# Turning attention's z and y rows with transposing transfers from SBUF to SBUF

## What is computed

```python
def _L0_xattn_ref(x, context, ...):           # 16 heads of 64, 77 keys a batch
    xn = _layernorm(x, ln_gamma, ln_beta)
    q = (xn @ w_q).reshape(B, SQ, NUM_HEADS, DIM_HEAD)
    k, v = jnp.split(context @ w_kv, 2, axis=-1)
...
    attn = jax.nn.softmax(jnp.einsum('bqhd,bkhd->bhqk', q * SCALE, k), axis=-1)
    out = jnp.einsum('bhqk,bkhd->bqhd', attn, v).reshape(B, SQ, INNER)
    return (out @ w_out + b_out) * jnp.tanh(gate[0])
def _L0_ffn_ref(inputs, gate_w, gate_b, expert_w, expert_b):
    gate_probs = jax.nn.softmax(x @ gate_w.T + gate_b, axis=-1)   # 8 experts and 2 null ones
    weights, selected = jax.lax.top_k(gate_probs, 2)
...
x = x + jnp.tanh(g_xattn[0]) * _L0_xattn_ref(_layernorm(x), ctx, ...)
x = x + jnp.tanh(g_ffn[0]) * _L0_ffn_ref(_layernorm(x), ...)
```

## Time and profile before

| | |
|---|---|
| median of 3 runs | 1773.74 us |
| the runs | 1767.39, 1773.74, 3117.3 us |
| span of the profiled execution | 1768.9 us |
| PE busy | 1483.3 us (84%) |
| DVE busy | 1438.9 us (81%) |
| POOL busy | 1089.4 us (62%) |
| ACT busy | 827.5 us (47%) |
| DMA queue of SP / of POOL, share of 16 engines | 23.5% / 13.0% |

### The profile page before, as it was taken

One profiled execution on the slowest core, in us unless ns is written; L12 is line 12 of the kernel. 1 busy time (PEld: TensorE's weight loads), 2 busy tenths in 40 slices (PEclk: granted clock), 3 DMA queues, 4 the chain that ended last, 5 costly groups with the idle time before them and its releaser, 6 DMA issues. The chain is left out here.

```text
span 1768.9 us, 38608 instructions
## 1 busy us (share of the span) xinstructions
PE 1483.3 (84%) x10329; PEld 815.2 (46%) x10330; DVE 1438.9 (81%) x3838; ACT 827.5 (47%) x1289; POOL 1089.4 (62%) x1029
## 2 busy tenths in 40 slices
PE   5675899999999999999999999999169998777775
PEld 3321455555555555555555555555034444333332
DVE  6766779999899999899999999997657777566664
ACT  6755454544544544554544544444134444333432
POOL 0620556766666766666766666665456665677775
PEclk9877999999999999999999999999579999899999
DMA  5986222132322142322132322111344443455553
GB/s 183 229 195 189 69 82 76 59 137 80 111 80 74 60 137 79 112 80 74 60 137 78 114 80 80 61 61 55 120 125 147 145 139 115 133 176 171 181 165 109
DMA packets 116661, 201.62 MB, mean 114 GB/s; under 512 B 23699, under 2 KB 51475, under 8 KB 115848
## 3 DMA queue, kind: packets, MB, share of 16 engines
q1 hardware_dynamic: 88520, 129.99, 23.5%
q0 software_dynamic: 28096, 71.08, 13.0%
HBM read 120.75 MB, written 83.07 MB: 115 GB/s over the span
## 5 line engine op out<-in xcount | busy, mean ns | idle before, releaser
L710 PE MATMUL mix<-u_sb,pT 128*128 128x512 f16 (+1 forms) x1920 | 429.8, 382 | 67.8 <-ACT pT L808 62.2
L676 PE MATMUL scores<-m_sb,zT 128*128 (+2 forms) x2304 | 413.7, 339 | 5.0 <-ACT zT L788 3.4
L1440 PE MATMUL out_bank<-w_parts,y_columns 128*128 x1440 | 335.6, 384 | 0.0
L710 PEld LDWEIGHTS mix<-u_sb,pT 128*128 128x128 f16 (+1 forms) x1920 | 184.3, 98 | 292.8 <-issue 76.2
L676 PEld LDWEIGHTS scores<-m_sb,zT 128*128 128x128 f16 x2304 | 224.3, 98 | 176.7 <-issue 8.3
L793 ACT ACTIVATE expd<-expd 128x385 f32<-128x385 f32 (+1 forms) x192 | 105.0, 547 | 325.1 <-DVE expd L891 325.1
L1462 ACT COPY y_columns<-yT_bank 128x1024 f16<-128x1024 f16 x120 | 121.5, 1012 | 245.9 <-PE yT_bank L1430 245.9
L1116 POOL DMA_INDIRECT table<-payload,row_i x128 | 192.9, 1507 | 44.6 <-issue 31.8
L1440 PEld LDWEIGHTS out_bank<-w_parts,y_columns 128*128 128x128 f16 x1440 | 137.5, 99 | 145.9 <-issue 6.7
L1380 POOL DMA_INDIRECT got_ring<-x_mid,token x120 | 127.0, 1058 | 96.4 <-DVE token L1493 67.8
L1430 PE MATMUL yT_bank<-ident,y_rows_parts 128*128 128x128 f16 x960 | 74.5, 221 | 107.2 <-issue 59.2
(11 more groups left out here) (147 smaller groups left out, 2644.2 us busy)
## 6 DMA issues: line engine op xcount, KB each, us to landing
x_ln<-in_x_dram SPq DMA_DIRECT2D x64, 256.0 KB, 2.6
x_res<-in_x_dram SPq DMA_DIRECT2D x64, 256.0 KB, 2.9
x_mid<-x_out SPq DMA_DIRECT2D x64, 256.0 KB, 2.1
out_dram<-x_out SPq DMA_DIRECT2D x64, 256.0 KB, 2.4
w_raw<-in_L_ffn_expert_w_dram SPq DMA_DIRECT2D x64, 128.0 KB, 2.6
m_dram<-m_stage SPq DMA_DIRECT2D x32, 231.0 KB, 5.2
u_dram<-m_sb SPq DMA_DIRECT2D x48, 154.0 KB
m_sb<-m_dram SPq DMA_DIRECT2D x3, 2464.0 KB, 9.0
```

The source lines that it names most:

```text
L676: last = pe.matmul(scores[k][:, 0:n], zT[:, s, zp, t, :], m, start=(t == 0 and (zp, mp) == PRODUCTS[0]), stop=(t == DT - 1 and (zp, mp) == ...
L710: last = pe.matmul(mix[:], pT[0:n, k, pp, :], u_sb[0:n, k, up, :], start=(k == 0 and (pp, up) == PRODUCTS[0]), stop=(k == KT - 1 and (pp, ...
L1440: last = pe.matmul(c.out_bank[s][:], yT[:, s, yp, t, :], w_parts[:, bass.ds(e, 1), t, wp, :].rearrange("p a n -> p (a n)"), start=(t == 0 ...
```

## The change

Both turns leave PE and ACT. SP issues one transposing transfer for z (`turn_z`) and one for y (`turn_y`) in each step, straight from `z_parts` and `y_parts` to `zT` and `yT` in SBUF, each for both parts at once; each raises one of two semaphores, by the tile's parity. `yT` gets a second buffer, and `zT_bank` goes. `score` and `gate` wait for these semaphores, and so do `split_z` and `split_y` before they write the parts again. `turn_z(i + 1)` and `turn_y(i - 3)` stand at the head of SP's step i. The first steps of the first batch are written out, since they have no y yet.

```diff
--- before.py
+++ after.py
@@ -440,7 +440,7 @@
         x_spread = sb("x_spread", [P, 2, 1])
         y = sb("y", [P, 2, D])
         y_parts = sb("y_parts", [P, 2, 2, D], F16)
-        yT = sb("yT", [P, 2, DT, P], F16)
+        yT = sb("yT", [P, 2, 2, DT, P], F16)
         gate_raw = sb("gate_raw", [P, DT, GATES])
         gate_scaled = sb("gate_scaled", [P, DT, GATES])
         gate_parts = sb("gate_parts", [P, DT, 2, GATES], F16)
@@ -480,7 +480,6 @@
         pT_bank = [psum(f"pT_bank{k}", [P, 4, 2, P], F16) for k in range(3)]
         gate_bank = pT_bank[2][:, 2:4].rearrange("p a b c -> p (a b c)").bitcast(F32)[:, 0:GATES]
         rank_bank = pT_bank[2][:, 2:4].rearrange("p a b c -> p (a b c)").bitcast(F32)[:, 16:16 + TOP_K * EXPERTS]
-        zT_bank = psum("zT_bank", [P, 2, DT, P], F16)
         mix = psum("mix", [P, D])
 
         affine_in = sem("affine_in")
@@ -500,8 +499,7 @@
         affine_done = sem("affine_done")
         z_hi_ready = sem("z_hi_ready")
         z_lo_ready = sem("z_lo_ready")
-        zT_summed = sem("zT_summed")
-        zT_ready = sem("zT_ready")
+        zT_in = [sem(f"zT_in{s}") for s in range(2)]
         scores_ready = sem("scores_ready")
         top_ready = sem("top_ready")
         less_ready = sem("less_ready")
@@ -525,8 +523,7 @@
         y_ready = sem("y_ready")
         y_hi_ready = sem("y_hi_ready")
         y_lo_ready = sem("y_lo_ready")
-        yT_summed = sem("yT_summed")
-        yT_ready = sem("yT_ready")
+        yT_in = [sem(f"yT_in{s}") for s in range(2)]
         gate_summed = sem("gate_summed")
         logits_ready = sem("logits_ready")
         choosing = sem("choosing")
@@ -587,11 +584,39 @@
                 sp.dma_start(w_raw[:, s, :], w_rows[bass.ds(i // 2, 1), s].rearrange("a p n -> (a p) n")).then_inc(
                     w_in[s], 16)
 
+            def turn_z(i, s):
+                sp.wait_ge(z_hi_ready, i + 1)
+                sp.nop(nofuse=True)
+                sp.wait_ge(z_lo_ready, i + 1)
+                sp.nop(nofuse=True)
+                if later(i, 2):
+
+                    sp.wait_ge(scores_ready, 3 * (i - 1))
+                sp.nop(nofuse=True)
+                sp.dma_start_transpose(out=zT[:, s].rearrange("p l t q -> p (l t) q"),
+                                       in_=z_parts[:, s].rearrange("p l d -> p (l d)")).then_inc(zT_in[s], 16)
+
+            def turn_y(i, s):
+                sp.wait_ge(y_hi_ready, i + 1)
+                sp.nop(nofuse=True)
+                sp.wait_ge(y_lo_ready, i + 1)
+                sp.nop(nofuse=True)
+                if later(i, 2):
+
+                    sp.wait_ge(gate_summed, i - 1)
+                sp.nop(nofuse=True)
+                sp.dma_start_transpose(out=yT[:, s].rearrange("p l t q -> p (l t) q"),
+                                       in_=y_parts[:, s].rearrange("p l d -> p (l d)")).then_inc(yT_in[s], 16)
+
             def store(i, s):
                 sp.dma_start(rows(x_mid, i), x_out[:, s, :]).then_inc(stored[s], 16)
                 sp.dma_start(rows(x_final, i), x_out[:, s, :]).then_inc(stored[s], 16)
 
-            def step(i, s, more=True, before=True):
+            def step(i, s, more=True, before=True, turns=True, turns_y=True):
+                if turns:
+                    turn_z(i + 1, 1 - s)
+                if turns_y:
+                    turn_y(i - 3, 1 - s)
                 if before:
 
                     sp.wait_ge(x_out_ready, i - 1)
@@ -617,13 +642,17 @@
 
 
                 i0 = b * TPB
-                step(i0, 0, before=not first)
+                step(i0, 0, before=not first, turns_y=not first)
                 if not first:
                     sp.wait_ge(mix_ready, i0)
                     for load in load_u(sp, u_sb, u_dram, b):
                         load.then_inc(u_in, 16)
-                step(i0 + 1, 1, before=not first)
-                with sp.Fori(0, TPB // 2 - 3) as q:
+                step(i0 + 1, 1, before=not first, turns_y=not first)
+                if first:
+                    step(2, 0, turns_y=False)
+                    for n in range(3, 6):
+                        step(n, n % 2)
+                with sp.Fori(2 if first else 0, TPB // 2 - 3) as q:
                     for k in range(2):
                         step(i0 + 2 * q + 2 + k, k)
                 if not last:
@@ -631,38 +660,29 @@
                         sp.wait_ge(scores_ready, 3 * i0)
                     load_m(sp, m_sb[:, bass.ds((b + 1) % 2, 1)], m_dram, b + 1).then_inc(m_in, 16)
                 for k in range(4):
-                    step(i0 + TPB - 4 + k, k % 2, more=not last)
+                    step(i0 + TPB - 4 + k, k % 2, more=not last, turns=not last or k < 3)
 
             for i in range(2):
                 sp.wait_ge(z_ready, i + 1)
                 load_x_ln(i + 2, i)
+            turn_z(0, 0)
             batch(0, first=True)
             with sp.Fori(1, BATCH - 1) as b:
                 batch(b)
             batch(BATCH - 1, last=True)
             for i in range(TILES - 2, TILES):
+                turn_y(i - 1, (i - 1) % 2)
                 sp.wait_ge(x_out_ready, i + 1)
                 store(i, i % 2)
+            turn_y(TILES - 1, (TILES - 1) % 2)
             for s in range(2):
                 sp.wait_ge(stored[s], 32 * TILES // 2)
 
         @block.tensor
         def _(pe):
-            def transpose_z(i, s):
-
-                pe.wait_ge(z_hi_ready, i + 1)
-                pe.wait_ge(z_lo_ready, i + 1)
-                pe.wait_ge(zT_ready, i)
-                if later(i, 4):
-                    pe.wait_ge(yT_ready, i - 3)
-                for part in range(2):
-                    for t in range(DT):
-                        last = pe.transpose(zT_bank[:, part, t, :], z_parts[:, s, part, t * P:(t + 1) * P], ident16[:])
-                last.then_inc(zT_summed, 1)
-
             def score(i, s):
 
-                pe.wait_ge(zT_ready, i + 1)
+                pe.wait_ge(zT_in[s], 8 * (i - s) + 16)
                 if later(i, TPB):
                     pe.wait_ge(m_in, 16 * (i // TPB))
                 for k in range(3):
@@ -712,18 +732,8 @@
                                              stop=(k == KT - 1 and (pp, up) == PRODUCTS[-1]))
                 last.then_inc(mix_ready, 1)
 
-            def transpose_y(i, s):
-                pe.wait_ge(y_hi_ready, i + 1)
-                pe.wait_ge(y_lo_ready, i + 1)
-
-                pe.wait_ge(zT_ready, i + 4 if not isinstance(i, int) or i + 4 <= TILES else TILES)
-                for part in range(2):
-                    for t in range(DT):
-                        last = pe.transpose(zT_bank[:, part, t, :], y_parts[:, s, part, t * P:(t + 1) * P], ident16[:])
-                last.then_inc(yT_summed, 1)
-
-            def gate(i):
-                pe.wait_ge(yT_ready, i + 1)
+            def gate(i, s):
+                pe.wait_ge(yT_in[s], 8 * (i - s) + 16)
                 if isinstance(i, int) and i == 0:
                     pe.wait_ge(gate_split, 3)
 
@@ -734,7 +744,7 @@
                 pe.wait_ge(pT_ready, 3 * (i + 3) if not isinstance(i, int) or i + 3 <= TILES else 3 * TILES)
                 for t in range(DT):
                     for yp, gp in PRODUCTS:
-                        last = pe.matmul(gate_bank, yT[:, yp, t, :], gate_parts[:, t, gp, :],
+                        last = pe.matmul(gate_bank, yT[:, s, yp, t, :], gate_parts[:, t, gp, :],
                                          start=(t == 0 and (yp, gp) == PRODUCTS[0]),
                                          stop=(t == DT - 1 and (yp, gp) == PRODUCTS[-1]))
                 last.then_inc(gate_summed, 1)
@@ -757,18 +767,13 @@
                     score(i, s)
                 if live(i - 1):
                     transpose_p(i - 1)
-                if live(i + 1):
-                    transpose_z(i + 1, 1 - s)
                 if live(i - 1):
                     mix_values(i - 1)
                 if live(i - 5):
                     rank(i - 5, 1 - s)
                 if live(i - 3):
-                    gate(i - 3)
-                if live(i - 2):
-                    transpose_y(i - 2, s)
-
-            transpose_z(0, 0)
+                    gate(i - 3, 1 - s)
+
             run(pe, step)
 
         @block.scalar
@@ -776,16 +781,10 @@
             def split_z(i, s):
 
                 act.wait_ge(affine_done, 2 * i + 2)
-                if not isinstance(i, int) or i >= 2:
-                    act.wait_ge(zT_summed, i - 1)
+                if later(i, 2):
+                    act.wait_ge(zT_in[s], 8 * (i - s))
+                    act.nop(nofuse=True)
                 act.copy(z_parts[:, s, 0, :], z[:, s, :]).then_inc(z_hi_ready, 1)
-
-            def copy_zT(i, s):
-                act.wait_ge(zT_summed, i + 1)
-                if not isinstance(i, int) or i >= 2:
-
-                    act.wait_ge(scores_ready, 3 * (i - 1))
-                act.copy(zT[:, s], zT_bank[:]).then_inc(zT_ready, 1)
 
             def exponent(i, s, k):
```

(14 more changed lines are left out.)

## The result

The changed kernel takes 1805.61 us, median of 4 runs (1803.24 to 1810.26), beside 1770.57 for the kernel before, run with it. The ratio is 1.0209, 95% interval 1.018 to 1.0238: slower, though the interval doesn't settle whether by more than 2%. The profiled execution spans 1804.4 us, against 1768.9 before, so 35.5 us are to be found.

What follows compares the result with a forecast made beforehand. The prediction took DVE to bound the attention stage. From the 1768.9 us trace span, 41 us for held steps and 5 us at the stage's ends gave 1815 us, own range 1805 to 1830, whole range 1755 to 1850.

Steps and rivals of the forecast that it cites:

- What bounds: Attention stage: DVE sets the pace, PE and ACT follow with about 1 us slack; direct gain 0 to 3 us.
- PE as the bound: Rival, attention stage: PE bounds, so 1.22 us a step come back whole or half; 1730 us at half; chance 0.05.
- The cast and z_low: Attention step: earlier ACT cast starts POOL's z_low 0.13 us before DVE's L1026, held; net 0.73 to 0.83 us a step.
- the rival by which a wait ahead of the cast makes it late by more than 0.13 us: Attention step: z_low starts after L1026, no stall, L975's 0.15 us a step won; 1766 us; chance 0.27.
- The transfers: SP's queue, z and y each step: 2 to 5 us each, hidden behind 16 us of slack, price 0.
- SP's issue: SP, each transposing transfer: about 0.4 us to issue, like its other issues, hidden, price 0.
- The slow rival: Attention stage: each transposing transfer takes 9.7 us, costing 7.2 us a step, 461 us, giving 2230; chance 0.20.
- The sum: Whole kernel: trace span 1768.9, plus 41 us for steps and 5 us at the stage's ends, gives 1815 us.
- some steps at batch starts not hit: Attention stage: z_low falls 0.2 to 0.5 us later against DVE there, so 55 of 64 steps were taken as hit.
- the steps' term: Attention stage: 55 held steps at 0.75 us each, 41 us in all.

Runs made afterwards that it cites:

- y alone: Kernel before with only y sent by a transposing transfer and no yT copy on ACT, z still turned by PE: 1822.28 us, ratio 1.0.
- early cast: Kernel before with two ACT calls exchanged, the cast of z ahead of the copy of zT, no transposing transfer: 1857.37 us, ratio 1.0179.
- filler: Changed kernel plus an unread ACT copy of about 1 us where the zT copy stood, transfers kept: 1827.79 us, ratio 1.002.
- placed pair: Changed kernel and kernel before, each with POOL's y_low waiting for row_i_ready and z_low for inverse_ready: ratios 0.9705 and 0.9738.
- placed kernel: Changed kernel with POOL's y_low waiting for row_i_ready and z_low for inverse_ready: 1788.59 us, ratio 0.9705.

## Why the prediction was right, step by step

**What bounds.** DVE did: PE's wait for pT grew to 2.2 us a step, as said (118.1 us over 52 waits), y alone won nothing an ordinary step, and each 0.16 or 0.87 us taken from DVE's list came back in the step. The prediction had PE as the bound at 0.05; it is not, save at a few batch starts (below).

**The cast and z_low.** Foreseen: z_low 0.13 us ahead of L1026, a stall to z_low's end, L975 freed, step up by 0.73 to 0.83 us. Measured: 0.13 us, 1.03 us long, L975 at 0.16, step up by 0.70. The early cast alone gave the same, and the rival by which a wait ahead of the cast makes it late by more than 0.13 us fell: the cast started 0.27 us after the copy ahead, as was read from the earlier trace rows.

**The transfers.** Foreseen 2 to 5 us and hidden: 3.2 us and hidden, as the filler shows. SP's issue was mis-sized, 1.23 us for 0.4, three times too low; it cost nothing in the stage, because SP is idle for most of a step. The slow rival's 9.7 us, as the usual price of a transfer, are seen nowhere: the longest landing of a y is 5.8 in the changed kernel, and y alone has one of 9.8 beside a median of 3.1. What the DMA engines moved, by slices of 0.225 us from 521 to 530 us of the changed kernel and of 0.375 us from 485 to 500:

```profile
GB/s 0 0 0 0 0 0 0 0 0 0 0 0 0 0 76 230 209 218 204 179 53 107 212 207 217 204 189 34 7 1 0 0 0 0 0 0 0 0 0 0
```

```profile
GB/s 0 0 0 0 0 0 0 0 0 0 0 0 0 180 212 205 106 160 209 206 127 6 0 0 0 0 0 0 0 240 399 350 377 77 208 404 361 33 0 0
```

The transfers of z and then of y go one after the other at 204 to 230 GB/s; the plain ones that follow at 495 us reach 350 to 404. The Trainium skill's two pages set against each other ahead of the result are both off here. "Advanced Engine Details and Errata", § X-Bar Transpose (TRN2), has transposing transfers as fast as plain ones, at 350 to 400 GB/s. By "VectorE: DVE Perf Modes", § The three transpose paths, 1309 ns a block would make 10.5 us of one transfer's eight blocks, an estimate; they land in 3.2.

**The sum.** Foreseen 1768.9 + 41 + 5 = 1815; measured 1804.4 in the profiled execution, 35.5 us more than before:

- The first "total" starts 2.0 us later (foreseen 2): before it PE waits for the first zT.

```profile
182.61 0.13 PEld L696 LDWEIGHTS scores<-m_sb,zT 128*128 128x128 f16 x2 [25.25 <-DMA zT<-z_parts]
```

- The 63 steps take 33.25 us more. This is the term that was mis-sized: 55 x 0.75 = 41 was foreseen. Fifty ordinary steps take 0.70 us more each, 34.8 in all, and the sixth and seventh 1.17 together. Against that, the first five are 0.72 us shorter in sum, the last two 0.85, and so are four at the starts of batches two and three: 18.07, 16.93, 17.93 and 16.92 us before, 17.18, 17.16, 17.18 and 17.16 in the changed kernel, 1.17 less in all. The prediction had some steps at batch starts not hit; they are hit, like all the others, and come out shorter because the kernel before lost time there that no longer shows. Its DVE waits there for PE, 1.45 and 1.30 us for mix and 0.65 us each time for scores:

```profile
469.18 0.69 DVE L915 SCALAR_TENSOR_TENSOR x_out<-mix,x_res 128x512 f32<-128x512 f32 x1 [1.45 <-PE mix L710]
...
476.25 0.56 DVE L889 TENSOR_REDUCE top<-scores 128x5 f32<-128x385 f32 x1 [0.65 <-PE scores L676]
...
734.63 0.69 DVE L915 SCALAR_TENSOR_TENSOR x_out<-mix,x_res 128x512 f32<-128x512 f32 x1 [1.30 <-PE mix L710]
```

The changed kernel's DVE waits for nothing in these four steps, but that cannot be put down to the transfers: the early cast, with all its work still on PE and ACT, has them at 17.18, 17.17, 16.31 and 17.17, as short as the changed kernel. Both have a DVE that is held longer in the ordinary step, and PE is in time there, but for one wait of 0.39 us in the early cast. Where nothing more is held, the removed work does pay: with y alone, at the old step, the four are 16.49, 16.45, 16.48 and 16.48, and the placed pair differs at these places too. The prediction read only the wait for scores (2.6 us) and left out the one for mix, 3.8 us from 250 to 1180 us.
- From the last "total" to the first load of the next stage 47.2 us for 44.3: 2.85 (foreseen 3). In SP's timeline of the changed kernel, and then of the kernel before:

```profile
1302.47 0.81 SPq L1202 DMA_DIRECT2D table_sb<-table  x2
```

```profile
1264.36 0.80 SPq L1213 DMA_DIRECT2D table_sb<-table  x2
```

- The rest of the program, whose instructions are the same, takes 501.9 us for 504.5. No run was made for these 2.6 us; the changed kernel's second profile has 502.3, and the executions of the kernel before within one set lie 7 us apart (1764.75 to 1771.6).

2.0 + 33.25 + 2.85 - 2.6 = 35.5. The forecast of 1815 is 10.6 us over this span: 7.75 of it in the steps' term (five ordinary steps fewer, 0.05 us less in each, and 1.6 us off in the others) and 2.6 in the part of the program that did not change.

## What to carry to other kernels

Work taken from an engine that waits anyway can still move time, by letting what is queued behind it start earlier: look at what that then runs beside, to a tenth of a microsecond. On the engine that sets the pace, read the duration of its smallest instructions. Here one that took 1.1 us where its equals take 0.16 was a stall by the other engine, and it was won back by a wait on that other engine, placed so that it always starts second. Here that was worth 3%, more than the change it was found with.

## What the runs showed of the hardware

- POOL's subtractions on SBUF and elementwise DVE instructions on SBUF hold each other, and the order of their starts decides which is held. DVE starting 0.07 to 0.13 us later waits to POOL's end even for 128x2 numbers (1.12 and 1.03 us for 0.16); the reduction L898 ran its 1.43 us beside z_low. The large ones are held as well (2.37 us for 1.44), and so is POOL when it is second (2.41 and 2.44 us for 1.16).
- A transposing transfer of 128x1024 f16 from SBUF to SBUF, 256 KB, lands in 3.2 us (3.0 to 5.8, once 9.8 with y alone), moves at 204 to 230 GB/s where plain ones reach 350 to 404, and takes SP 1.23 us to issue (median; 0.75 for y's in the placed kernel), the plain pair above 0.81 for two. The 128 of them are 135,168 packets more in SP's queue, 1056 each, and raise the DMA share of the stretch from 0.26 to 0.41.
- PE's granted clock, as a mean of 200 us, was 0.95 in the changed kernel from 500 to 700 us (PE busy 175.5) and 1.00 from 300 to 500 (busy 170.0), with ordinary steps of 17.17 us in both; in before it was 1.00 and 0.99. From 250 to 1180 us a mix product took 396 ns on average, 381 in before. Neither shows in the step.
